# Recursive feature interaction on one core: the D groups moved ahead of c1, their copies shared by two engines, three tile loads put behind the D stores, and a lead of 7 chunks

## The chip, the cores and the metric

The kernel runs on one core of one Trainium2 chip. The metric is the device time of one execution in microseconds; less is better. The kernel before takes 185.95 us (median of 3 runs, 185.75 to 186.69).

## What is computed

The reference takes an input of 512 examples, 40 features and 16 dimensions, and three layers of weights. Each layer multiplies the input pairwise with the layer before and contracts the pairs with a weight tensor; the hidden rows of all three layers are summed over the 16 dimensions and go through one linear layer:

```python
base = inputs
curr = base
logit = []
for Wk, bk in zip(Ws, bs):
    z = jnp.einsum('bid,bjd->bdij', base, curr)
    curr = jnp.einsum('bdij,ijh->bhd', z, Wk) + bk[None, :, None]
    logit.append(curr)
pooled = jnp.sum(jnp.concatenate(logit, axis=1), axis=-1)
out = pooled @ lin_w + lin_b
```

Here `inputs` is 512 x 40 x 16, the weights are 40 x 40 x 100 and 40 x 100 x 100 (twice), and the output is 512 x 1.

## The kernel before

The columns (512 examples x 16 dimensions) are cut into 8 units of 1024 columns. Within a unit the products of pairs of features, `z`, are made in 7 chunks of 126 rows each, so there are 56 chunks, numbered m = 0 to 55. For each chunk VectorE (DVE) multiplies a tile `x_a` with a tile `x_b` into the buffer `xb_z` (function `form`), ScalarE (ACT) rounds it to `z_high` (`round_high`), and DVE takes the rest, `z_low` (`split`). TensorE (PE) then uses the chunk twice, each time in six matmuls of 512 columns: once with the weights `wc` (function `c1_chunk`, PSUM tiles `c1_ps`, called c_ps in the rows), once with the weights `wq` (`q_chunk`, PSUM tiles `q_ps`). Below, c7 is `c1_chunk` of chunk 7 and q0 is `q_chunk` of chunk 0. A split needs the rounded tile; c m needs both. For units 0 and 1 the program is written out; the later units run in hardware loops of two units.

The weights `wq` are not an input. Layers 2 and 3 are folded into them at the start: PE multiplies the last layer's weights into a vector `v` (`v_piece`, `turn_v`), then multiplies `w1_post` with it in five D groups (`d_group`, into two halves of the PSUM tile q_ps). Each group is copied to SBUF (`copy_d`, tile `w2_d`, called w_d in the rows), stored to memory in six transfers of the SP queue and one of GpSimd (POOL) (`store_d`, line L159), and read back in another layout in twelve gathers (`gather_d`, line L153) into `pair_sb`. Gathers of piece 0 hold the weights of chunks 0 and 1, those of piece 1 the chunks 2 to 6. Each piece is then added, rounded and split in three instructions per part (`first_weights` on DVE for chunks 0 and 1, lines L279 to L284; POOL for chunks 2 and 3 and for 4 to 6, lines L419 to L424).

In unit 0 the tiles `x_b` of chunks 1 to 6 are made by PE (`select_xb`); from unit 1 on they are loaded from memory by SP (`load_xb`, 512 KB each, line L171), each into the slot of `xb_z` that the split of seven chunks before has freed (semaphore `low_done`). Tile k of unit 1 belongs to chunk 7 + k.

Every engine executes its own stream in program order. SP's stream is the order in which its transfers are issued, and each semaphore wait in it holds back everything behind it. The constant `LAG` says how many chunks PE's c work is ahead of its q work: after the first `LAG` chunks of c, PE alternates q(m - LAG), c(m). Both kinds of chunk share 14 slots for `z`, which q frees.

Of the kernel before, what the change touches and what calls it, by code (L numbers as in the profile page):

```python
# [16 lines left out]
SLOTS = 2 * C  # L17
LAG = 8
BODY = 2 * C
PRODUCT_AT = 20  # L20
C1_AT = 3 * C - LAG

# [37 lines left out]
def build(nc, xa, xw, w0_pairs, w1x, w2h, small, out):  # L60
    fp32, f32r = mybir.dt.float32, mybir.dt.float32r
    ALU, ACT = mybir.AluOpType, mybir.ActivationFunctionType

    with ExitStack() as ctx:
# [3 lines left out]
        def sem(name):  # L68
            return ctx.enter_context(nc.semaphore(name))
# [96 lines left out]
        def _(sp):  # L166
# [3 lines left out]
            def load_xb(u, c):  # L170
                sp.dma_start(xb_z[:, c, :], xw[c:c + 128, bass.ds(u * N, N)]).then_inc(xb_loaded[c], 16)  # L171
# [47 lines left out]
            for c in range(4, C):  # L219
                sp.wait_ge(low_done, c + 1)  # L220
                load_xb(1, c)
# [13 lines left out]
        def _(dve):  # L235
# [38 lines left out]

            def first_weights():

                cols = slice(PREP_CUTS[0] * J, PREP_CUTS[1] * J)
                dve.wait_ge(dpair_loaded[0], 16 * sum(g[2] == 0 for g in GATHER))
                nc.vector.tensor_tensor(q_sides[0:K, 0, cols], q_sides[0:K, 0, cols], q_sides[0:K, 1, cols],  # L279
                                        ALU.add).then_inc(wq_sums, 1)  # L280
                dve.wait_ge(wq_sums, 1)
                nc.vector.tensor_copy(wq_high[0:K, cols], q_sides[0:K, 0, cols]).then_inc(wq_highs, 1)
                dve.wait_ge(wq_highs, 1)
# [35 lines left out]
        def _(act):  # L319
# [71 lines left out]
        def _(pool):  # L391
# [21 lines left out]
            for i in range(1, len(PREP_CUTS) - 1):
                cols = slice(PREP_CUTS[i] * J, PREP_CUTS[i + 1] * J)
                if PREP_CUTS[i] in WQ_CUTS:
                    piece = WQ_CUTS.index(PREP_CUTS[i])
                    pool.wait_ge(dpair_loaded[piece], 16 * sum(g[2] == piece for g in GATHER))
                    pool.wait_ge(wq_ready, 1)
                nc.gpsimd.tensor_tensor(q_sides[0:K, 0, cols], q_sides[0:K, 0, cols], q_sides[0:K, 1, cols],  # L419
                                        ALU.add).then_inc(wq_sums, 1)  # L420
                pool.wait_ge(wq_sums, i + 1)
                nc.gpsimd.tensor_copy(wq_high[0:K, cols], q_sides[0:K, 0, cols]).then_inc(wq_highs, 1)
                pool.wait_ge(wq_highs, i + 1)
                nc.gpsimd.tensor_tensor(wq_low[0:K, cols], q_sides[0:K, 0, cols], wq_high[0:K, cols].bitcast(fp32),  # L424
                                        ALU.subtract).then_inc(wq_ready, 1)

        @block.tensor
        def _(pe):
# [77 lines left out]
            def d_group(g):  # L506
# [130 lines left out]
```

## Time and profile before

| | |
|---|---|
| runs, median of 3 | 185.95 us |
| profiled execution, its own time | 186.29 us |
| its span, first to last instruction | 184.5 us |
| PE busy | 175.8 us (95%) |
| DVE busy | 151.8 us (82%) |
| ACT busy | 73.9 us (40%) |
| POOL busy | 16.2 us (9%) |

The span leaves 1.8 us of the execution's time outside of it. Busy time of PE is that of matmuls; the other engines work beside it. Times in the rows below are counted from the start of the span.

### The profile page before, as it was taken

What the parts mean: (1) busy time and instruction counts of PE and PEld (TensorE: products, weight loads), DVE (VectorE), ACT (ScalarE), POOL (GpSimd) and SP (SyncE); (2) the same over time, 40 slices, a digit from 0 to 9 for tenths busy, and PEclk for the clock granted to TensorE, in tenths of its full rate; (3) what the DMA queues carried; (4) which work ended last, traced back from release to release, by engine and by line L of the source; (5) the groups of instructions that cost most, each with busy time, mean ns of one, the idle gap of its engine ahead of it and who ended that gap; (6) DMA issues with size and microseconds to landing.
All of it is one profiled execution on the core that took longest, in us unless ns stands there. A gap on an engine that the chain in (4) does not pass through costs nothing.

```text
span 184.5 us, 2573 instructions
## 1 busy us (share of the span) xinstructions
PE 175.8 (95%) x814; PEld 118.7 (64%) x814; DVE 151.8 (82%) x135; ACT 73.9 (40%) x79; POOL 16.2 (9%) x21
## 2 busy tenths in 40 slices
PE   7798998869999999999999999999999999999994
PEld 2364474546677777777777777777777777777760
DVE  0699698869999999999999999999999999300622
ACT  2554664124444624462446244534453445002001
POOL 3670010087000000000000000000000000000000
PEclk9999999999999999999999999999999999999999
DMA  6999997999797739774986597659765200000000
GB/s 192 379 409 411 412 219 218 231 406 397 230 324 233 234 122 321 247 227 124 331 230 228 126 322 235 223 135 329 228 219 128 99 0 0 0 0 4 0 0 0
DMA packets 11845, 37.71 MB, mean 204 GB/s; under 512 B 2305, under 2 KB 2941, under 8 KB 11838
## 3 DMA queue, kind: packets, MB, share of 16 engines
q1 hardware_dynamic: 11538, 37.38, 62.1%
q0 software_dynamic: 48, 0.16, 0.3%
q10 hardware_dynamic: 252, 0.09, 0.3%
q8 instruction: 4, 0.07, 0.2%
q14 instruction: 3, 0.02, 0.0%
HBM read 36.28 MB, written 1.33 MB: 204 GB/s over the span
## 4 chain that ended last, share of the span: by engine, by line
PE 79%; DMA 8%; SPq 3%; POOL 3%; issue 2%; DVE 1%; ACT 1%; DVEq 0%; ACTq 0%
PE q_ps L434 39%; PE c_ps L434 36%; DMA pair_sb<-d_dram 3%; DMA pair_sb<-w_pairs 3%; DMA d_dram<-w_d 2%; PE q_ps L518 2%; SPq L153 2%; POOL pair_sb L401 1%; POOL wq_low L424 1%; PE q_ps L443 1%; POOL wc_low L406 1%; DVE xb_z L246 1%; ACT z_high L324 1%; SPq L159 1%; PE c_ps L565 1%
## 5 line engine op out<-in xcount | busy, mean ns | idle before, releaser
L324 ACT ACTIVATE z_high<-xb_z 126x1024 fp32r<-126x1024 f32 x56 | 59.2, 1060 | 73.0 <-DVE xb_z L246 69.3
L253 DVE TENSOR_TENSOR z_low<-xb_z,z_high 126x1024 fp32r<-126x1024 f32 x56 | 68.9, 1232 | 1.1 <-ACT z_high L324 0.8
L246 DVE TENSOR_TENSOR xb_z<-x_a,xb_z 126x1024 f32<-126x1024 f32 x50 | 62.1, 1242 | 8.3 <-DMA xb_z<-xw 8.3
L434 PE MATMUL q_ps<-z_high,wq_high 126*101 126x512 f32 x108 | 34.1, 396 | 3.0 <-POOL wq_low L424 1.5
L434 PE MATMUL c_ps<-z_high,wc_high 126*101 126x512 f32 x112 | 35.5, 398 | 0.2 <-issue 0.2
L434 PE MATMUL c_ps<-z_high,wc_low 126*101 126x512 f32 x112 | 35.0, 394 | 0.0
L434 PE MATMUL c_ps<-z_low,wc_high 126*101 126x512 f32 x112 | 35.0, 394 | 0.0
L434 PE MATMUL q_ps<-z_high,wq_low 126*101 126x512 f32 x108 | 33.8, 394 | 0.0
L434 PE MATMUL q_ps<-z_low,wq_high 126*101 126x512 f32 x108 | 33.7, 393 | 0.0
L434 PEld LDWEIGHTS q_ps<-z_high,wq_high 126*101 126x101 f32 x108 | 17.7, 165 | 10.8 <-POOL wq_low L424 2.0
L434 PEld LDWEIGHTS c_ps<-z_high,wc_high 126*101 126x101 f32 x112 | 18.0, 165 | 9.0 <-issue 1.6
L434 PEld LDWEIGHTS c_ps<-z_high,wc_low 126*101 126x101 f32 x112 | 18.5, 165 | 7.5
L434 PEld LDWEIGHTS c_ps<-z_low,wc_high 126*101 126x101 f32 x112 | 18.5, 165 | 7.4
L434 PEld LDWEIGHTS q_ps<-z_high,wq_low 126*101 126x101 f32 x108 | 17.9, 166 | 7.3
L434 PEld LDWEIGHTS q_ps<-z_low,wq_high 126*101 126x101 f32 x108 | 17.8, 165 | 7.2
L261 DVE TENSOR_TENSOR w_post<-q_ps,w_post 101x1024 f32<-101x1024 f32 x7 | 8.5, 1216 | 12.0 <-PE q_ps L434 12.0
L331 ACT ACTIVATE w_post<-c_ps 101x1024 f32<-101x1024 f32 x8 | 8.1, 1010 | 14.1 <-PE c_ps L434 14.1
L263 DVE TENSOR_TENSOR acc<-acc,w_post 101x1024 f32<-101x1024 f32 x7 | 8.6, 1226 | 0.2
L485 PE MATMUL q_ps<-warm_sb 128*128 128x512 bf16 x20 | 6.2, 483 | 1.4 <-POOL warm_sb L393 1.4
L267 DVE TENSOR_TENSOR w_post<-q_ps,w_post 101x256 f32<-101x256 f32 (+1 forms) x3 | 1.4, 508 | 5.2 <-PE q_ps L443 5.2
L388 ACT ACTIVATE out_sb<-c_ps,const_sb 1x512 f32<-1x512 f32 x1 | 0.7, 678 | 12.2 <-PE c_ps L568 12.2
L485 PEld LDWEIGHTS q_ps<-warm_sb 128*128 128x128 bf16 x20 | 2.3, 121 | 4.7 <-issue 2.2
(56 smaller groups left out, 66.1 us busy)
## 6 DMA issues: line engine op xcount, KB each, us to landing
xb_z<-xw SPq DMA_DIRECT2D x50, 512.0 KB, 4.5
x_a<-xa SPq DMA_DIRECT2D x8, 512.0 KB, 5.0
w_d<-w2h SPq DMA_DIRECT2D x4, 512.0 KB, 7.4
w_post<-w1x SPq DMA_DIRECT2D x3, 512.0 KB, 10.0
d_dram<-w_d SPq DMA_DIRECT2D x4, 252.5 KB, 4.3
w_post<-w1x SPq DMA_DIRECT2D x1, 562.5 KB, 12.7
pair_sb<-d_dram SPq DMA_DIRECT2D x6, 82.9 KB
pair_sb<-w_pairs SPq DMA_DIRECT2D x1, 404.0 KB, 5.4
```

The lines of the kernel that those rows point to most:

```text
L153: eng.dma_start(q_sides[P * t:P * (t + 1), side, c0 * J:c1 * J].rearrange("p (c j) -> p c j", j=J), src).then_inc(dpair_loaded[piece], 16)
L159: eng.dma_start(d_dram[r0:r1, column * J:(column + n) * J], w2_d[DR * upper + r0:DR * upper + r1, first * J:(first + n) * J]).then_inc(sto ...
L246: nc.vector.tensor_tensor(xb_z[0:K, c, :], x_a[0:K, u % 2, :], x_b, ALU.mult).then_inc(z_done, 1)
L253: nc.vector.tensor_tensor(z_low[0:K, m % SLOTS, :], xb_z[0:K, c, :], z_high[0:K, m % SLOTS, :].bitcast(fp32), ALU.subtract).then_inc(low_d ...
L261: nc.vector.tensor_tensor(prod, q_ps[u % 2][0:J, :], c1_sb[u % 2], ALU.mult).then_inc(q_psum_free, 1)
L263: nc.vector.tensor_tensor(acc[:, :], acc[:, :], prod, ALU.add).then_inc(acc_done, 1)
L324: nc.scalar.activation(z_high[0:K, m % SLOTS, :], xb_z[0:K, m % C, :], ACT.Copy).then_inc(high_done, 1)
L331: nc.scalar.activation(c1_sb[u % 2], c1_ps[u % 2][0:J, :], ACT.Copy).then_inc(c1_copied, 1)
L401: nc.gpsimd.tensor_tensor(side[:, :, 0, :], side[:, :, 0, :], side[:, :, 1, :], ALU.add).then_inc(wc_sums, 1)
L434: last = nc.tensor.matmul(ps[0:J, h * B:(h + 1) * B], w[0:K, c * J:(c + 1) * J], z[0:K, slot, h * B:(h + 1) * B], start=(c == 0 and k == 0 ...
L485: nc.tensor.matmul(warm_ps, warm_sb[:, 0:128], warm_sb[:, :], start=True, stop=True)
L518: last = nc.tensor.matmul(d_ps[g % 2][0:DR, 0:n], v_sb[:, :], w1_post[0:J, first:first + n], start=True, stop=True)
```

## The change

Six things change together.

1. PE: the D groups 0 to 4 stand ahead of c1; `select_xb(6)` stands between groups 1 and 2 instead of ahead of group 4.
2. The copies of groups 1 and 3 go from ACT to DVE (`copy_d` of DVE), with a semaphore of its own; all that waited for `dgroup_copied` now waits for both.
3. SP: tiles 0 and 1 of unit 1, which stood ahead of the D stores, come behind them: tile 0 behind the last store, tile 1 where tile 3 was (ahead of the gathers of piece 1), tile 2 between the third and the fourth gather of piece 1, tile 3 behind them.
4. `LAG` is 7 instead of 8: c0 to c6, then q0, c7, q1, c8, q2, c9 and so on.
5. DVE: the split of chunk 6 stands ahead of the form of chunk 7, `first_weights(0)` ahead of the split of chunk 7 (before: ahead of the split of chunk 8), and the weights of chunks 2 and 3 are made by DVE too (`first_weights(1)`), behind the split of chunk 8, which stands behind the form of chunk 9. POOL keeps the weights of chunks 4 to 6 alone.
6. ACT issues its three gathers ahead of the rounding of chunk 7 instead of chunk 8.

```diff
-LAG = 8
+LAG = 7
-C1_AT = 3 * C - LAG
+C1_AT = 2 * C - 1
-PREP_AT = 9
-GATHER_AT = 8
+PREP_AT = (7, 9)
+GATHER_AT = 7
...
             load_xa(1, 1)
-            for c in range(2):
-                sp.wait_ge(low_done, c + 1)
-                load_xb(1, c)
-            sp.wait_ge(dgroup_copied, 2)
+            sp.wait_ge(dgroup_copied, 1)
+            sp.wait_ge(dgroup_copied_dve, 1)
             store_d(sp, 0, LEFT, 0, 2 * GI, d_stored)
...
             store_d(sp, 0, LEFT + 4 * GI, 4 * GI, LOWER - 4 * GI, d_stored)
-            sp.wait_ge(low_done, 3)
-            load_xb(1, 2)
+            sp.wait_ge(low_done, 1)
+            load_xb(1, 0)
...
                 if piece == 1 and (side, t) == (0, 0):
-                    sp.wait_ge(low_done, 4)
-                    load_xb(1, 3)
+                    sp.wait_ge(low_done, 2)
+                    load_xb(1, 1)
+                if piece == 1 and (side, t) == (1, 1):
+                    sp.wait_ge(low_done, 3)
+                    load_xb(1, 2)
...
+            def copy_d(g):
+                dve.wait_ge(dgroup_done, g + 1)
+                nc.vector.tensor_copy(w2_d[:, g * GI * J:(g + 1) * GI * J], d_ps[g % 2]).then_inc(dgroup_copied_dve, 1)
...
                 for m in range(m0, m0 + BODY):
+                    if m == 5:
+                        copy_d(1)
+                    if m == C:
+                        split(it, C - 1)
                     form(it, m)
+                    if m == 5:
+                        copy_d(3)
...
-                    if m == PREP_AT:
-                        first_weights()
-                    if m > 1:
+                    if m == PREP_AT[0]:
+                        first_weights(0)
+                        split(it, C)
+                    elif m > 1 and m != C + 1:
                         split(it, m - 1)
+                    if m == PREP_AT[1]:
+                        first_weights(1)
...
             d_group(0)
             d_group(1)
-            c1_chunk(0, 1)
+            select_xb(6)
             d_group(2)
             d_group(3)
-            select_xb(6)
             d_group(4)
-            for m in range(2, LAG):
+            for m in range(1, LAG):
                 c1_chunk(0, m)
```

SP's stream before, from the second load of `x_a` to the last tile of unit 1 (xb_z<-xw is a tile load, d_dram<-w_d a store, pair_sb<-d_dram a gather):

```order
L168 DMA x_a<-xa 128x1024
L171 DMA xb_z<-xw 128x1024 x2
L159 DMA d_dram<-w_d 64x1010 x2
L159 DMA d_dram<-w_d 32x909
L159 DMA d_dram<-w_d 64x1010 x2
L159 DMA d_dram<-w_d 64x101
L171 DMA xb_z<-xw 128x1024
L153 DMA pair_sb<-d_dram 42x202 x3
L171 DMA xb_z<-xw 128x1024
L153 DMA pair_sb<-d_dram 42x505
L153 DMA pair_sb<-d_dram 42x5x101
```

The same place of SP's stream in the changed kernel, up to the fourth gather of piece 1 (line numbers are those of the changed kernel):

```order
L170 DMA x_a<-xa 128x1024
L161 DMA d_dram<-w_d 64x1010 x2
L161 DMA d_dram<-w_d 32x909
L161 DMA d_dram<-w_d 64x1010 x2
L161 DMA d_dram<-w_d 64x101
L173 DMA xb_z<-xw 128x1024
L155 DMA pair_sb<-d_dram 42x202 x3
L173 DMA xb_z<-xw 128x1024
L155 DMA pair_sb<-d_dram 42x505
L155 DMA pair_sb<-d_dram 42x5x101
L155 DMA pair_sb<-d_dram 42x505
L173 DMA xb_z<-xw 128x1024
```

Before, four tiles of unit 1 (0 to 3) stand ahead of the gathers of piece 1; now there are two (0 and 1) and a third (tile 2) in the middle of them.

DVE's stream before, from the form of chunk 7 to the form of chunk 11 (L246 is a form, L253 a split, L279 to L284 the weights of chunks 0 and 1):

```order
L246 TENSOR_TENSOR xb_z<-x_a,xb_z 126x1024
L253 TENSOR_TENSOR z_low<-xb_z,z_high 126x1024
L246 TENSOR_TENSOR xb_z<-x_a,xb_z 126x1024
L253 TENSOR_TENSOR z_low<-xb_z,z_high 126x1024
L246 TENSOR_TENSOR xb_z<-x_a,xb_z 126x1024
L279 TENSOR_TENSOR pair_sb<-pair_sb 126x202
L282 CAST wq_high<-pair_sb 126x202
L284 TENSOR_TENSOR wq_low<-pair_sb,wq_high 126x202
L253 TENSOR_TENSOR z_low<-xb_z,z_high 126x1024
L246 TENSOR_TENSOR xb_z<-x_a,xb_z 126x1024
L253 TENSOR_TENSOR z_low<-xb_z,z_high 126x1024
L246 TENSOR_TENSOR xb_z<-x_a,xb_z 126x1024
```

DVE's stream in the changed kernel, from the form of chunk 7 to the split of chunk 9 (L250 is a form, L257 a split, L287 to L292 weights):

```order
L250 TENSOR_TENSOR xb_z<-x_a,xb_z 126x1024
L287 TENSOR_TENSOR pair_sb<-pair_sb 126x202
L290 CAST wq_high<-pair_sb 126x202
L292 TENSOR_TENSOR wq_low<-pair_sb,wq_high 126x202
L257 TENSOR_TENSOR z_low<-xb_z,z_high 126x1024
L250 TENSOR_TENSOR xb_z<-x_a,xb_z 126x1024 x2
L257 TENSOR_TENSOR z_low<-xb_z,z_high 126x1024
L287 TENSOR_TENSOR pair_sb<-pair_sb 126x202
L290 CAST wq_high<-pair_sb 126x202
L292 TENSOR_TENSOR wq_low<-pair_sb,wq_high 126x202
L250 TENSOR_TENSOR xb_z<-x_a,xb_z 126x1024
L257 TENSOR_TENSOR z_low<-xb_z,z_high 126x1024
```

The forms of chunks 8 and 9 now stand together, ahead of the split of chunk 8, and the second set of weights stands between that split and the form of chunk 10.

## Rows read from the trace of the kernel before

**Rows 1.** The page: span, engines (busy us, share, instructions)

```profile
span 184.5 us, 2573 instructions
PE 175.8 (95%) x814; PEld 118.7 (64%) x814; DVE 151.8 (82%) x135; ACT 73.9 (40%) x79; POOL 16.2 (9%) x21
```

**Rows 2.** The chain that ended last: start, us, what

```profile
23.51 4.53 DMA d_dram<-w_d
...
32.04 5.49 DMA pair_sb<-d_dram
...
38.71 1.68 POOL wq_low L424
...
57.70 1.39 PE q_ps L434 x6
```

**Rows 3.** Timeline of PE: start, us, what, count [idle before, releaser]

```profile
18.27 0.70 PE L434 MATMUL c_ps<-z_high,wc_high 126*101 126x512 f32 x2
...
19.80 0.64 PE L518 MATMUL q_ps<-w_post,v_sb 101*64 101x505 f32 x1
...
21.65 0.73 PE L476 MATMUL q_ps<-z_high,select_r 126*128 126x512 f32 x2
22.31 0.39 PE L518 MATMUL q_ps<-w_post,v_sb 101*64 101x101 f32 x2
...
29.98 0.69 PE L434 MATMUL c_ps<-z_high,wc_high 126*101 126x512 f32 x2 [0.18 <-issue]
...
33.10 0.70 PE L434 MATMUL q_ps<-z_high,wq_high 126*101 126x512 f32 x2 [1.50 <-DVE wq_low L284]
...
40.44 0.71 PE L434 MATMUL q_ps<-z_high,wq_high 126*101 126x512 f32 x2 [1.50 <-POOL wq_low L424]
...
47.69 0.68 PE L434 MATMUL c_ps<-z_high,wc_high 126*101 126x512 f32 x2
```

**Rows 4.** Timeline of DVE

```profile
17.48 1.23 DVE L253 TENSOR_TENSOR z_low<-xb_z,z_high 126x1024 fp32r<-126x1024 f32 x1
18.63 1.21 DVE L246 TENSOR_TENSOR xb_z<-x_a,c_ps 126x1024 f32<-126x1024 f32 x1
...
31.88 0.37 DVE L279 TENSOR_TENSOR pair_sb<-pair_sb 126x202 f32<-126x202 f32 x1 [0.87 <-DMA pair_sb<-d_dram]
...
32.88 1.22 DVE L253 TENSOR_TENSOR z_low<-xb_z,z_high 126x1024 fp32r<-126x1024 f32 x1
34.78 1.23 DVE L246 TENSOR_TENSOR xb_z<-x_a,xb_z 126x1024 f32<-126x1024 f32 x1 [0.69 <-DMA xb_z<-xw]
...
41.39 1.87 DVE L246 TENSOR_TENSOR xb_z<-x_a,xb_z 126x1024 f32<-126x1024 f32 x1
```

**Rows 5.** Timeline of ACT: the copy of D group 3

```profile
21.77 0.59 ACT L338 ACTIVATE w_d<-q_ps 128x505 f32<-128x505 f32 x1 [0.26 <-PE q_ps L521]
```

**Rows 6.** Timeline of POOL

```profile
40.35 1.82 POOL L419 TENSOR_TENSOR pair_sb<-pair_sb 126x303 f32<-126x303 f32 x1
```

**Rows 7.** Timeline of SP's issues: start of the first, us to the last's end, what, count

```profile
24.20 0.58 SPq L171 DMA_DIRECT2D xb_z<-xw  x1
28.11 1.19 SPq L153 DMA_DIRECT2D pair_sb<-d_dram  x3
29.34 0.37 SPq L171 DMA_DIRECT2D xb_z<-xw  x1
29.76 2.67 SPq L153 DMA_DIRECT2D pair_sb<-d_dram  x6
```

**Rows 8.** Line L159, the store issued at 22.38: time from issue to landing

```profile
DMA to landing us min/median/max: 3.5/3.5/3.5
```

**Rows 9.** Line L171, tile 3 of unit 1, issued at 29.34: issue to landing

```profile
DMA to landing us min/median/max: 5.3/5.3/5.3
```

**Rows 10.** Line L171, tile 4 of unit 1, issued at 32.47: issue to landing

```profile
DMA to landing us min/median/max: 6.1/6.1/6.1
```

**Rows 11.** Line L171, tile 5 of unit 1, issued at 32.91: issue to landing

```profile
DMA to landing us min/median/max: 7.0/7.0/7.0
```

More of the change, by code:

```diff
@@ L202, in _ @@
             store_d(sp, 0, LEFT + F, 0, RIGHT, d_stored, (32, DR))
-            sp.wait_ge(dgroup_copied, 4)
+            sp.wait_ge(dgroup_copied, 2)
+            sp.wait_ge(dgroup_copied_dve, 2)
             store_d(sp, 0, LEFT + 2 * GI, 2 * GI, 2 * GI, d_stored)
             store_d(sp, 1, LEFT + LOWER + 2 * GI, 2 * GI, 2 * GI, d_stored)
-            sp.wait_ge(dgroup_copied, NG)
+            sp.wait_ge(dgroup_copied, 3)
             store_d(sp, 0, LEFT + 4 * GI, 4 * GI, LOWER - 4 * GI, d_stored)
-            sp.wait_ge(low_done, 3)
-            load_xb(1, 2)
+            sp.wait_ge(low_done, 1)
+            load_xb(1, 0)
             sp.wait_ge(equals_cleared, 1)
@@ L214, in _ @@
                 if piece == 1 and (side, t) == (0, 0):
-                    sp.wait_ge(low_done, 4)
-                    load_xb(1, 3)
+                    sp.wait_ge(low_done, 2)
[3 more added lines that the diff above has]
+                    load_xb(1, 2)
                 if side == 0 or piece > 0:
                     gather_d(sp, side, t, piece)
-            for c in range(4, C):
+            for c in range(3, C):
                 sp.wait_ge(low_done, c + 1)
@@ L273, in split_x, with first_weights @@
                                         ALU.subtract).then_inc(xa_split, 1)
-            def first_weights():
-                cols = slice(PREP_CUTS[0] * J, PREP_CUTS[1] * J)
-                dve.wait_ge(dpair_loaded[0], 16 * sum(g[2] == 0 for g in GATHER))
+            def copy_d(g):
+                dve.wait_ge(dgroup_done, g + 1)
+                nc.vector.tensor_copy(w2_d[:, g * GI * J:(g + 1) * GI * J], d_ps[g % 2]).then_inc(dgroup_copied_dve, 1)
+            def first_weights(i):
+                cols = slice(PREP_CUTS[i] * J, PREP_CUTS[i + 1] * J)
+                dve.wait_ge(dpair_loaded[i], 16 * sum(g[2] == i for g in GATHER))
                 nc.vector.tensor_tensor(q_sides[0:K, 0, cols], q_sides[0:K, 0, cols], q_sides[0:K, 1, cols],
                                         ALU.add).then_inc(wq_sums, 1)
-                dve.wait_ge(wq_sums, 1)
+                dve.wait_ge(wq_sums, i + 1)
                 nc.vector.tensor_copy(wq_high[0:K, cols], q_sides[0:K, 0, cols]).then_inc(wq_highs, 1)
-                dve.wait_ge(wq_highs, 1)
+                dve.wait_ge(wq_highs, i + 1)
                 nc.vector.tensor_tensor(wq_low[0:K, cols], q_sides[0:K, 0, cols], wq_high[0:K, cols].bitcast(fp32),
@@ L360, in _ @@
             copy_d(0)
-            copy_d(1)
             round_high(0, 4)
             copy_d(2)
-            copy_d(3)
             copy_d(4)
-            act.wait_ge(dgroup_copied, NG)
+            act.wait_ge(dgroup_copied, 3)
+            act.wait_ge(dgroup_copied_dve, 2)
             for m in range(5, BODY):
@@ L410, in _ @@
             pool.wait_ge(equals_cleared, 1)
-            pool.wait_ge(dgroup_copied, 4)
+            pool.wait_ge(dgroup_copied, 2)
+            pool.wait_ge(dgroup_copied_dve, 2)
             store_d(pool, 1, 0, UPPER - LEFT, LEFT, d_stored_pool, (0, 32))
[L413 to L425, printed above, removed]
+            cols = slice(PREP_CUTS[2] * J, PREP_CUTS[3] * J)
+            pool.wait_ge(dpair_loaded[1], 16 * sum(g[2] == 1 for g in GATHER))
+            nc.gpsimd.tensor_tensor(q_sides[0:K, 0, cols], q_sides[0:K, 0, cols], q_sides[0:K, 1, cols],
+                                    ALU.add).then_inc(last_sums, 1)
+            pool.wait_ge(last_sums, 1)
+            nc.gpsimd.tensor_copy(wq_high[0:K, cols], q_sides[0:K, 0, cols]).then_inc(last_highs, 1)
+            pool.wait_ge(last_highs, 1)
+            nc.gpsimd.tensor_tensor(wq_low[0:K, cols], q_sides[0:K, 0, cols], wq_high[0:K, cols].bitcast(fp32),
+                                    ALU.subtract).then_inc(last_ready, 1)
         @block.tensor
@@ L460, in q_chunk @@
                 u, c = divmod(m, C)
-                if m in PREP_CUTS[:-1]:
+                if m in PREP_CUTS[:2]:
                     pe.wait_ge(wq_ready, PREP_CUTS.index(m) + 1)
+                if m == PREP_CUTS[2]:
+                    pe.wait_ge(last_ready, 1)
                 if c == 0:
@@ L513, in d_group @@
                     pe.wait_ge(w1_loaded[W1_CUTS.index(g)], 16)
-                if g >= 2:
-                    pe.wait_ge(dgroup_copied, g - 1)
+                if g in (2, 4):
+                    pe.wait_ge(dgroup_copied, g // 2)
+                if g == 3:
+                    pe.wait_ge(dgroup_copied_dve, 1)
                 n = (GI if g < NG - 1 else 1) * J
```

2 lines of the change are left out of this document (added).

## Prediction

> **What bounds the kernel now.** I read the page first: PE is busy for 175.8 of 184.5 us [rows 1], so PE's own work is the bound, and only its gaps can be won. The chain that ended last [rows 2] shows where they are: from 40.44 on it is nothing but PE, chunk behind chunk at 1.39 us, and ahead of that it runs through the D stores (23.51 to 28.04), the gathers of piece 1 (32.04 to 37.53) and POOL's weights. PE's timeline [rows 3] gives the two gaps that matter: 1.50 us ahead of q0 at 33.10 and 1.50 ahead of q2 at 40.44. The gap ahead of c7 is 0.18, so c6 ended at 29.80. Behind 40.44 PE loses only crumbs: c12 starts at 47.69, five chunks later, 7.25 us where 5 x 1.39 are 6.95.
>
> Nothing in the change alters the amount of PE work. So I ask only when PE gets to which chunk. A lead of 7 has its own marks: at q0 one chunk of c less is done than before (c7), so the new kernel is level with the old one when q0 starts at 33.10 - 1.39 = 31.71, c8 at 40.44 - 2 x 1.39 = 37.66, and q2 at 39.05. For c9 I count back from c12, whose mark is 47.69 + 1.39 = 49.08: six chunks (c9, q3, c10, q4, c11, q5) are 8.34, so the mark of c9 is **40.74**. What PE is late there is late at the end.
>
> **D groups.** c1 costs 19.80 - 18.27 = 1.53 us of PE and goes behind the groups; the selection for chunk 6 costs 22.31 - 21.65 = 0.66 and stands now ahead of group 2 [rows 3]. So groups 2 and 3 come 0.87 earlier, and c6 still ends at 29.80, since the same things are done by then. Group 3's copy started at 21.77 and took 0.59 [rows 5]; now it can start at 20.90, on DVE. The trace has no copy of 505 columns on DVE; the bounds are 0.37 (202 columns) and 1.21 (1024 columns) [rows 4], and a straight line between them gives 0.68, which I take. It ends at 21.58 instead of 22.36: 0.78 earlier (1.1 to 0.25 by the bounds). The copy of group 1 stands where the form of chunk 5 started (18.63) and pushes it by 0.7, which is hidden: c5 is needed near 27. ACT loses two copies and has idle time anyway.
>
> **D stores.** The last store's landing ended the wait at 28.04. Two tiles, 1 MB, no longer stand ahead of the stores. That helps the first three, but the gathers wait for the last, issued after group 3's copy. The first store behind that copy landed 3.5 us after its issue [rows 8], the last 4.53 after the end of its own [rows 2], because three others go beside it. Nothing in the change thins these, so I shift the last landing by 0.78 only: the gathers start at 28.11 - 0.78 = 27.33 [rows 7]. If the last store too landed 3.5 after its issue, they would start at 26.3; if the copies gain only 0.25, at 27.9.
>
> **First weights and q0.** Before, gathers at 28.11 gave a landing at 31.88 (3.77 later), DVE's three instructions took 1.00 until its next one, and PE started 1.22 after the landing [rows 3, 4]. Now: landing 31.10, q0 at **32.32**. That is 0.61 behind its mark of 31.71, a wait of 2.5 us where 1.5 stood: the gain of 0.78 doesn't pay for the chunk c7 that no longer fills the hole. c7 runs behind q0; its split ends near 33.3, in time. Tile 0 takes tile 2's place in the queue (24.20 - 0.78, landed near 28.7 with the 5.3 of rows 9); DVE has time for chunk 7's form before 31.10.
>
> **The tiles.** This is the larger term. Tile 1 stands where tile 3 stood: issued at 29.34 - 0.78 = 28.56, and with its 5.3 [rows 9] landed at 33.86. Before, tile 3 landed at 34.64, the six gathers of piece 1 at 37.53, tile 4 at 38.57 and tile 5 at 39.91 [rows 2, 7, 9 to 11]. So six gathers cost 2.89 behind a tile, and a tile 1.0 to 1.3. Now tile 2 comes behind three gathers: 33.86 + 1.45 + 1.3 = 36.6 if the queue is strictly one behind the other, and 33.86 + 1.3 = 35.2 if the gathers run beside it. Some of tile 3's 5.3 was such overlap, so I take the middle, **35.9**. Piece 1 then lands near 37.4 to 38.1, no earlier than before: its issue gains 0.78 and loses a tile.
>
> The Trainium skill (DMA: Bandwidth & Descriptors, Queues, rings and completion order) says that each DMA engine takes the descriptors of one queue in the order of the ring. By that rule tile 2 can't pass the three gathers, 36.6 would hold, and the loss below would be 2.0 instead of 1.3 us; the landings here fit it but don't decide between the two.
>
> **DVE behind the tiles.** In its stream form 8, form 9, split 8, the second weights, form 10 and split 9 stand in this order. Form 9 needs tile 2, and c8 needs split 8 behind it. A form or split costs 1.15 from start to start, the weights 1.00 [rows 4]. From tile 2's landing: form 9 and split 8 2.3 (c8 at 38.3, against its mark of 37.66), weights 1.0, form 10 and split 9 2.3, and 0.1 until PE starts: c9 5.7 after tile 2. At 35.9 that is 41.6. q2 is done by then (38.3 + 2 x 1.39 = 41.1), so the splits decide.
>
> **POOL beside DVE.** POOL begins the weights of chunks 4 to 6 as soon as piece 1 has landed, with the addition of 303 columns (1.82 us [rows 6]), while DVE does the second weights and form 10. In the old trace a form beside that instruction took 1.87 instead of 1.21 [rows 4]. I charge 0.4 on the path, between nothing and twice 0.66. c9 starts at **42.0**, 1.26 us behind its mark.
>
> Here the Trainium skill (SBUF — State Buffer, Who interferes with whom) has a stricter rule: a VectorE instruction with two SBUF inputs and a GpSimd one that reads SBUF exclude each other for the whole of one instruction. By it DVE could lose up to 1.8 in one piece instead of 0.66, and the loss would grow to about 2.7. The 1.87 us form is slower, but less than that.
>
> **Behind c9.** DVE makes a chunk in 2.3 us, PE uses one in 2.78, so DVE gets ahead again and nothing more is lost. POOL has lost the smaller part of its weights (202 of 505 columns) and starts the rest at once, so q4 doesn't wait. At the end seven chunks of q follow the last c instead of eight; PE's sum is the same. DVE's five added instructions (two copies, three for the weights of chunks 2 and 3) all fall into the start and are counted above.
>
> **Sum.** +1.26 us, rounded to +1.25. The profiled execution took 186.29 against 184.5 of span; it is 0.34 above the median of 185.95. The forecast is on the median: 185.95 + 1.25 = **187.2 us**. A measurement of this kernel can tell about 0.5%, 0.93 us, from no change.
>
> **The rivals.**
>
> - *Same, chance 0.34.* Tile 2 is not far behind tile 1: at 35.2 c9 comes at 40.9, with POOL's 0.4 at 41.3, 0.56 late, 186.5 us. All of tile 2's landings from 34.1 to 35.2 or so end within 0.93 us. For it speaks that gathers of short rows may leave the queue free for tiles; against it, that tile 3 before took 5.3 with fewer gathers ahead of it. That the stores come no earlier (gathers at 27.9) belongs to the slower side, at about 187.8.
> - *Faster, chance 0.14.* The mechanism is the emptied queue: without the 1 MB ahead, every store lands 3.5 after issue, the gathers start at 26.3 and piece 0 lands at 30.07. Tile 1 is then issued at 27.5 and lands at 32.8; tile 2 1.0 later at 33.8, and piece 1 at 30.07 + 5.65 = 35.7, if the extra tile fits into the idle time of the DMA engines. c9 comes at 39.5, 1.2 before its mark: 184.7 us. It decides from tile 2 landed by 34.1 on. Against it: the last stores waited for each other, not for the tiles.
> - *Slower, chance 0.52.* The forecast, with tile 2 from 35.6 to 36.6 or later, 186.9 to 188.6 us; its upper end holds the exclusive lock too.
>
> The range leaves out most of the faster case and the rarest mishaps: 185.1 to 188.7.
>
> **What would show it.** D stores: the last copy on DVE ends near 21.6, the gathers start near 27.3. q0 starts near 32.3 behind a wait of 2.5. DVE waits for tiles ahead of form 8 (33.9) and form 9 (35.9), and PE waits ahead of c8 and c9 for DVE, not ahead of q2 for POOL. The prediction is wrong if the gathers start before 26.5 or form 9 before 34.2; then the gain of the early D groups reaches PE. It is also wrong, upward, if PE's longer waits lower its granted clock, of which the old trace shows nothing.

## The result, and the profile after

The changed kernel takes **189.0 us** (median of 4 runs, 188.62 to 189.32) against 186.32 us for the kernel before (median of 4 runs, 185.75 to 187.09): the ratio is 1.014, 95% interval 1.0093 to 1.0188. The profiled execution took 189.32 us with a span of 187.5, so 3.0 us more span than before. The sign was forecast, the size wasn't: 2.7 us instead of 1.25, and 189.0 us, where 187.2 was forecast, lies above the range of 185.1 to 188.7.

From the page of the changed kernel, the lines that answer to [rows 1], and the granted clock in 40 slices:

```profile
span 187.5 us, 2572 instructions
PE 177.8 (95%) x814; PEld 119.9 (64%) x814; DVE 153.2 (82%) x140; ACT 72.8 (39%) x77; POOL 11.4 (6%) x18
PEclk9999999699999999999999999999999999999999
```

PE's busy time has grown by 2.0 us with the same 814 matmuls, and the eighth slice of the clock (32.8 to 37.5 us) shows a 6. PE's timeline in the changed kernel, D group 3, then the first row of q0, c7, c8, q2, c9 and c12, to be held against [rows 3]:

```profile
20.50 0.64 PE L535 MATMUL q_ps<-w_post,v_sb 101*64 101x505 f32 x1 [0.19 <-DMA w_post<-w1x]
...
32.95 1.01 PE L447 MATMUL q_ps<-z_high,wq_high 126*101 126x512 f32 x2 [2.69 <-DVE wq_low L292]
...
35.46 1.06 PE L447 MATMUL c_ps<-z_high,wc_high 126*101 126x512 f32 x2
...
39.15 0.68 PE L447 MATMUL c_ps<-z_high,wc_high 126*101 126x512 f32 x2 [0.23 <-DVE z_low L257]
...
41.40 0.70 PE L447 MATMUL q_ps<-z_high,wq_high 126*101 126x512 f32 x2 [0.64 <-DVE wq_low L292]
...
43.76 0.68 PE L447 MATMUL c_ps<-z_high,wc_high 126*101 126x512 f32 x2 [0.75 <-DVE z_low L257]
...
52.11 0.62 PE L447 MATMUL c_ps<-z_high,wc_high 126*101 126x512 f32 x2
```

c9 starts at 43.76; its mark was 40.74, so PE is 3.02 us behind there, and the span ends 3.0 us later: behind c9 nothing more is lost (c12 at 52.11, 3.03 behind its mark of 49.08). Of this, 0.30 us is there before any of PE's work differs: PE starts D group 0 at 16.73 in this profile and at 16.43 in that of the kernel before. It is probably no work of the change, since e3 below, with the same streams up to that point, starts it at 16.11. Without it c9 is 2.72 late, and the medians differ by 2.7. The rest of the loss is made ahead of c9, and the last brackets name DVE: its weights ahead of q0 and q2, its splits ahead of c8 and c9.

DVE's timeline in the changed kernel (L250 forms, L257 splits, L281 the copies of D groups, L287 to L292 weights), to be held against [rows 4]:

```profile
21.62 0.68 DVE L281 COPY w_d<-q_ps 128x505 f32<-128x505 f32 x1 [0.88 <-PE q_ps L538]
...
31.73 0.37 DVE L287 TENSOR_TENSOR pair_sb<-pair_sb 126x202 f32<-126x202 f32 x1 [1.01 <-DMA pair_sb<-d_dram]
...
33.86 1.22 DVE L250 TENSOR_TENSOR xb_z<-x_a,xb_z 126x1024 f32<-126x1024 f32 x1
36.64 1.22 DVE L250 TENSOR_TENSOR xb_z<-x_a,xb_z 126x1024 f32<-126x1024 f32 x1 [1.56 <-DMA xb_z<-xw]
37.78 1.22 DVE L257 TENSOR_TENSOR z_low<-xb_z,z_high 126x1024 fp32r<-126x1024 f32 x1
38.91 1.00 DVE L287 TENSOR_TENSOR pair_sb<-pair_sb 126x202 f32<-126x202 f32 x1
39.95 0.38 DVE L290 CAST wq_high<-pair_sb 126x202 fp32r<-126x202 f32 x1
40.36 0.98 DVE L292 TENSOR_TENSOR wq_low<-pair_sb,wq_high 126x202 fp32r<-126x202 f32 x1
41.27 1.21 DVE L250 TENSOR_TENSOR xb_z<-x_a,xb_z 126x1024 f32<-126x1024 f32 x1
```

POOL's timeline beside it, for [rows 6], and SP's issues of the first gathers, for [rows 7]:

```profile
38.21 1.48 POOL L432 TENSOR_TENSOR pair_sb<-pair_sb 126x303 f32<-126x303 f32 x1 [14.64 <-DMA pair_sb<-d_dram]
39.75 0.46 POOL L435 CAST wq_high<-pair_sb 126x303 fp32r<-126x303 f32 x1
40.29 0.83 POOL L437 TENSOR_TENSOR wq_low<-pair_sb,wq_high 126x303 fp32r<-126x303 f32 x1
```

```profile
27.63 1.19 SPq L155 DMA_DIRECT2D pair_sb<-d_dram  x3
28.87 0.37 SPq L173 DMA_DIRECT2D xb_z<-xw  x1
```

Form 8 follows split 7 at once, where the text expected a wait for tile 1 until 33.9: tile 1, issued at 28.87, landed 4.5 us later at 33.4. Form 9 waits for tile 2 until 36.64, a split behind it, and then come the second weights: the same three instructions that take 0.99 us to the next one at 31.73 take 2.36 (38.91 to 41.27), with POOL's three beside them. Tile 2's issue at 30.62 and its landing:

```profile
L173 SPq DMA_DIRECT2D xb_z<-xw x1: 371/371/371, 30.6 to 30.6; - x1
...
DMA to landing us min/median/max: 5.9/5.9/5.9
```

The clock is in the busy times by stretch (busy us of PE, PEld, DVE, ACT, POOL, then granted clock, DMA share, GB/s):

```profile
30.00:33.00 3.00, 0.31 (x3) 0.06 (x1) 1.92 (x5) 1.06 (x1) 0.00 (x0) 1.00 0.87 259
33.00:36.00 3.00, 3.00 (x8) 2.03 (x9) 2.08 (x2) 0.89 (x1) 0.00 (x0) 0.53 1.05 265
36.00:37.00 1.00, 1.00 (x5) 0.72 (x4) 0.36 (x1) 0.17 (x1) 0.00 (x0) 0.71 1.11 174
```

After the wait of 2.69 us the granted clock is 0.50, that is 1.2 GHz, from 33.2 until about 36.6. q0 and c7 together take 4.41 us (32.95 to 37.36) instead of 2.78. Two explanations stand: **the DVE theory** (tile 2 and the slowed weights set c9, and the clock's loss falls into a wait) and **the clock theory** (the 1.63 us of q0 and c7 are the missing part of the loss).

### The profile page after: what moved, and what is told of

Same layout as the page of the kernel before. It is cut to its first block, busy times and chain, and to the rows that moved or that the text cites. A ratio compares the mean times of both kernels' runs of the same rounds, so it can differ in the third digit from the quotient of the medians.

```text
span 187.5 us, 2572 instructions
## 1 busy us (share of the span) xinstructions
PE 177.8 (95%) x814; PEld 119.9 (64%) x814; DVE 153.2 (82%) x140; ACT 72.8 (39%) x77; POOL 11.4 (6%) x18
## 4 chain that ended last, share of the span: by engine, by line
PE 75%; DMA 13%; SPq 6%; DVE 2%; issue 1%; ACT 0%; DVEq 0%
PE q_ps L447 38%; PE c_ps L447 35%; DMA w_post<-w1x 7%; DMA xb_z<-xw 4%; DMA d_dram<-w_d 2%; SPq L155 2%; SPq L181 1%; SPq L185 1%; SPq L173 1%; PE q_ps L456 1%; SPq L177 1%; DVE xb_z L250 1%; DVE z_low L257 1%; PE q_ps L535 1%; SPq L161 1%
## 5 line engine op out<-in xcount | busy, mean ns | idle before, releaser
L250 DVE TENSOR_TENSOR xb_z<-x_a,xb_z 126x1024 f32<-126x1024 f32 x50 | 61.0, 1219 | 10.1 <-DMA xb_z<-xw 10.1
L257 DVE TENSOR_TENSOR z_low<-xb_z,z_high 126x1024 fp32r<-126x1024 f32 x56 | 68.4, 1224 | 0.9 <-ACT z_high L341 0.9
L500 PE MATMUL q_ps<-warm_sb 128*128 128x512 bf16 x20 | 6.7, 512 | 1.4 <-POOL warm_sb L409 1.4
```

Source lines behind the costliest of these rows:

```text
L250: nc.vector.tensor_tensor(xb_z[0:K, c, :], x_a[0:K, u % 2, :], x_b, ALU.mult).then_inc(z_done, 1)
L257: nc.vector.tensor_tensor(z_low[0:K, m % SLOTS, :], xb_z[0:K, c, :], z_high[0:K, m % SLOTS, :].bitcast(fp32), ALU.subtract).then_inc(low_d ...
L500: nc.tensor.matmul(warm_ps, warm_sb[:, 0:128], warm_sb[:, :], start=True, stop=True)
```

## The experiments

Each ran beside the kernel before on the same chip; "ratio" is to that kernel, with its 95% interval. Reading single microseconds from one profile needs care: c2 starts anywhere from 22.36 to 23.34 in them, and D group 0, which stands ahead of everything that differs on PE, anywhere from 16.11 to 16.73 (16.43 before). Where two are compared, I count from c2's start, and for the D groups from the start of group 0.

### e3_fill_clock: PE kept at work through the wait

```diff
             for m in range(1, LAG):
                 c1_chunk(0, m)
+            pe.wait_ge(dgroup_copied, 3)
+            pe.wait_ge(dgroup_copied_dve, 2)
+            for _ in range(FILL):          # 10
+                warm()
```

> The changed kernel with ten added matmuls on zeros (2.2 us of work, into PSUM that is free then) between c6 and q0, so that PE doesn't stand still for 2.7 us. Theory: the clock stays at 2.4 GHz, q0 to q1 end 1.6 us earlier, but c8 still waits for split 8 until 39.1 and the end doesn't move (within 0.4 us). Rival (clock): the time falls by 1.6 us to about 187.4.

Measured: 188.79 us, ratio 1.0164 (1.0116 to 1.0213). The clock stayed at 1.00 in the whole span and q0 and c7 took 2.96 us instead of 4.41. PE's and DVE's timelines show where that went:

```profile
37.94 0.68 PE L448 MATMUL c_ps<-z_high,wc_high 126*101 126x512 f32 x2 [1.94 <-DVE z_low L258]
```

```profile
35.43 1.23 DVE L251 TENSOR_TENSOR xb_z<-x_a,xb_z 126x1024 f32<-126x1024 f32 x1 [1.59 <-DMA xb_z<-xw]
36.57 1.22 DVE L258 TENSOR_TENSOR z_low<-xb_z,z_high 126x1024 fp32r<-126x1024 f32 x1
37.71 1.00 DVE L288 TENSOR_TENSOR pair_sb<-pair_sb 126x202 f32<-126x202 f32 x1
```

What q0 and c7 won is a wait of 1.94 us ahead of c8, for the same split behind the same tile. The 1.6 us that the clock theory promised are not in the time. From c2 to c9 it is 20.02 us instead of 20.61, but tile 2 landed 0.6 us earlier in this profile too (5.2 us after its issue at 30.14). The mean clock was 1.00 in three of the six executions (188.18, 188.35 and 189.08 us) and 0.99 in the others (188.50, 189.17 and 190.42), where all four of the changed kernel have 0.99; too few to price it to some tenths. e1 below, with the clock up and no gain either, says the same: the clock theory is out as the missing part of the loss.

### e2_tile2_ahead: tile 2 ahead of all gathers of piece 1

```diff
                 if piece == 1 and (side, t) == (0, 0):
                     sp.wait_ge(low_done, 2)
                     load_xb(1, 1)
-                if piece == 1 and (side, t) == (1, 1):
                     sp.wait_ge(low_done, 3)
                     load_xb(1, 2)
```

> The changed kernel; tile 2 is issued right behind tile 1, ahead of all six gathers of piece 1. Theory: tile 2 lands near 34.8 instead of 36.5, split 8 ends near 37.2, and then the gathers' landing (38.2, unchanged) holds DVE's second weights; c9 comes near 43.0, 0.7 us earlier, time about 188.3. Rival (clock): c8 can't start before q1 ends at 38.9, so nothing at c8; a gain of at most 0.25 us.

Measured: 188.5 us, ratio 1.0147 (1.0095 to 1.0199). Form 9 no longer waits: forms 8 and 9 run from 34.28 to 36.63 and split 8 starts at 36.62, and from c2 to c9 it is 19.44 us (23.19 to 42.63) instead of 20.61. That gain of 1.17 us is hardly in the time, whose interval holds the changed kernel's ratio. It moves the profile as the DVE theory says; the time alone doesn't prove it. POOL and DVE begin their additions side by side here:

```profile
37.71 0.84 POOL L431 TENSOR_TENSOR pair_sb<-pair_sb 126x303 f32<-126x303 f32 x1 [14.09 <-DMA pair_sb<-d_dram]
```

```profile
37.77 1.01 DVE L286 TENSOR_TENSOR pair_sb<-pair_sb 126x202 f32<-126x202 f32 x1
```

### e1_serial_weights: POOL waits until DVE's second weights are done

```diff
             pool.wait_ge(dpair_loaded[1], 16 * sum(g[2] == 1 for g in GATHER))
+            pool.wait_ge(wq_ready, 2)
```

> The changed kernel; POOL's weights of chunks 4 to 6 wait until DVE's second weights are done. Theory (DVE's chain behind tile 2 sets c9, and POOL beside it costs 1.36 us on the second weights): those three instructions take 1.0 us again instead of 2.36, POOL's work then falls beside form 10 and split 9 and slows them by 0.4 to 0.9, so c9 starts 0.5 to 1.0 us earlier than in the changed kernel (43.76) and the time falls by as much, to about 188.2. Rival (PE's clock at its lower level after the long wait is what costs): no change of the time, since q0 and its wait are as before.

Measured: 189.15 us, ratio 1.0169 (1.0125 to 1.0214), no gain. DVE's and POOL's timelines:

```profile
38.40 0.36 DVE L287 TENSOR_TENSOR pair_sb<-pair_sb 126x202 f32<-126x202 f32 x1
38.80 0.27 DVE L290 CAST wq_high<-pair_sb 126x202 fp32r<-126x202 f32 x1
39.10 0.37 DVE L292 TENSOR_TENSOR wq_low<-pair_sb,wq_high 126x202 fp32r<-126x202 f32 x1
39.38 1.22 DVE L250 TENSOR_TENSOR xb_z<-x_a,xb_z 126x1024 f32<-126x1024 f32 x1
40.52 1.86 DVE L257 TENSOR_TENSOR z_low<-xb_z,z_high 126x1024 fp32r<-126x1024 f32 x1
42.30 1.45 DVE L250 TENSOR_TENSOR xb_z<-x_a,xb_z 126x1024 f32<-126x1024 f32 x1
43.67 1.86 DVE L257 TENSOR_TENSOR z_low<-xb_z,z_high 126x1024 fp32r<-126x1024 f32 x1
```

```profile
39.63 1.67 POOL L433 TENSOR_TENSOR pair_sb<-pair_sb 126x303 f32<-126x303 f32 x1 [16.84 <-DVE wq_low L292]
41.36 1.31 POOL L436 CAST wq_high<-pair_sb 126x303 fp32r<-126x303 f32 x1
42.75 1.70 POOL L438 TENSOR_TENSOR wq_low<-pair_sb,wq_high 126x303 fp32r<-126x303 f32 x1
```

The first half of the expectation held: alone, the weights take 0.98 us to the next instruction. But POOL's work then lies beside the splits, and three long instructions give back 0.65 + 0.24 + 0.65 = 1.54 us (over 1.21). From c2 to c12 it is 28.94 us (22.36 to 51.30), in the changed kernel 28.96. So POOL's 303 columns cost DVE 1.4 to 1.5 us in either place; DVE has no idle time in either. The clock stayed at 1.00 in this profile, behind a wait of 2.19 us ahead of q0 and one of 2.55 ahead of c8, and q0 and c7 took 2.89 us: that didn't make the kernel faster either.

### e7_pool_weights: POOL makes the weights of chunks 2 and 3 again

```diff
-                    if m == PREP_AT[1]:
-                        first_weights(1)
...
+            low = slice(PREP_CUTS[1] * J, PREP_CUTS[2] * J)
+            nc.gpsimd.tensor_tensor(q_sides[0:K, 0, low], q_sides[0:K, 0, low], q_sides[0:K, 1, low],
...
```

> The changed kernel with the weights of chunks 2 and 3 made by POOL again, ahead of those of chunks 4 to 6. Theory: DVE saves the 2.36 us of its second weights, form 10 starts when tile 3 has landed (39.3), and POOL's longer work slows form 10 and the splits by some 1.5 us in all; c9 near 42.8, time 0.5 to 1.0 us below the changed kernel. Rival (q2 waits longer for POOL): q2 not before 41.5 and no gain.

Measured: 188.82 us, ratio 1.0118 (1.0067 to 1.017). The rival was the nearer: q2 starts at 42.95, behind a wait of 1.68 us for POOL, in a profile that is the longest of the six executions (189.91 us; the shortest took 187.18). The interval holds the changed kernel's ratio, so neither a gain nor a loss from this part, undone alone, is shown.

### e5_tiles_back: the tiles issued as before

```diff
+            for c in range(2):
+                sp.wait_ge(low_done, c + 1)
+                load_xb(1, c)
             sp.wait_ge(dgroup_copied, 1)
...
-            sp.wait_ge(low_done, 1)
-            load_xb(1, 0)
+            sp.wait_ge(low_done, 3)
+            load_xb(1, 2)
...
-                    sp.wait_ge(low_done, 2)
-                    load_xb(1, 1)
+                    sp.wait_ge(low_done, 4)
+                    load_xb(1, 3)
```

(Tile 2 in the middle of the gathers goes too; the loop behind them starts at tile 4.)

> The changed kernel with the tiles of unit 1 issued as before: 0 and 1 ahead of the stores, 2 behind them, 3 ahead of piece 1. Theory (the tiles' new place is the larger loss): DVE no longer waits for tiles ahead of form 8 and form 9, split 8 ends near 37, c9 starts near 41.0, and the time is within 0.7 us of the kernel before, 186.5. Rival (the lead of 7 or the order of DVE's work is the loss): time stays at 188 or above.

Measured: 187.35 us, ratio 1.0086 (1.0052 to 1.0121). PE's waits in it:

```profile
32.33 0.70 PE L447 MATMUL q_ps<-z_high,wq_high 126*101 126x512 f32 x2 [1.89 <-DVE wq_low L292]
...
41.59 0.68 PE L447 MATMUL c_ps<-z_high,wc_high 126*101 126x512 f32 x2 [0.50 <-DVE z_low L257]
```

DVE doesn't wait for tiles, split 8 ends at 36.82, and c9 starts 0.85 behind its mark; the span is 185.4, 0.9 above before. The theory had 186.5 us, the rival 188 or more; the time lies between. Put back, the tiles take 0.54% off the ratio's 1.4%, about 1.0 us, though the two intervals overlap; in the two profiles c9 comes 2.2 us earlier. It is the largest gain of the parts that I undid alone, but a loss of 0.86% remains. The slowed weights are still there:

```profile
36.73 1.00 DVE L287 TENSOR_TENSOR pair_sb<-pair_sb 126x202 f32<-126x202 f32 x1
```

The next form starts at 39.09, 2.36 us behind this row. From 31.12, where the first weights start, to the end of split 9 at 41.44 DVE never stops, so here its own work sets c9. How the 0.86% divides between the lead and the weights no run shows.

### e6_lead8: a lead of 8 in the changed kernel

```diff
-LAG = 7
+LAG = 8
```

> The changed kernel with a lead of 8. Theory: the lead of 7 limits the damage of the late tiles. With 8, c7 must come ahead of q0 and waits for its split (near 34), and c9 stands ahead of q2 and waits for split 9 (43.7) with one chunk less done; the time is 1.4 us above the changed kernel, about 190.4. Rival (the lead is neutral, or a loss of its own): the same as the changed kernel within 0.4 us, or less.

Measured: 190.29 us, ratio 1.0226 (1.0183 to 1.027), as expected (190.4). c7 starts at 34.67 and c9, now ahead of q2, at 43.74 behind split 9. With the tiles late, the lead of 7 saves 1.3 us by the medians, 1.6 by the ratios.

### e9_lead7_alone: a lead of 7 in the kernel before

```diff
-LAG = 8
+LAG = 7
...
-C1_AT = 3 * C - LAG
+C1_AT = 2 * C - 1
```

> The kernel before with a lead of 7 and nothing else. Theory (the marks: at equal times of q0 and q2 a lead of 7 has one chunk less behind it): q0 still waits for the first weights until 33.1, now 2.9 us, q2 for POOL's until 40.4, and one chunk more is left then; 1.4 us slower, 187.3. PE's clock falls after the long wait, which is hidden ahead of q2. Rival (the lead only reorders PE's work and is neutral): within 0.4 us of before.

Measured: 186.94 us, ratio 1.0062 (1.0024 to 1.0101); 1.16 us, expected 1.4. PE's one long wait:

```profile
33.44 0.70 PE L434 MATMUL q_ps<-z_high,wq_high 126*101 126x512 f32 x2 [3.48 <-DVE wq_low L284]
```

The wait ahead of q0 is 3.48 us, and q2 starts at 40.65 where its mark is 39.05. It doesn't wait for POOL, as I had expected: the clock fell to 0.50 behind the long wait, and q0 to c8 took 7.21 us where four chunks at full clock are 5.56. POOL's weights were ready at 40.16, so at most some 0.5 us of the delay is the clock's and the rest would have been a wait. The rest of the kernel runs through. A chunk taken out of a hole comes back as most of a chunk of time at the end, as the marks say.

### e10_tiles_alone: the tiles' new places in the kernel before

```diff
-            for c in range(2):
-                sp.wait_ge(low_done, c + 1)
-                load_xb(1, c)
             sp.wait_ge(dgroup_copied, 2)
...
-            sp.wait_ge(low_done, 3)
-            load_xb(1, 2)
+            sp.wait_ge(low_done, 1)
+            load_xb(1, 0)
```

(Tiles 1 and 2 stand among the gathers as in the change.)

> The kernel before with the tiles in the changed kernel's places (0 behind the stores, 1 ahead of piece 1, 2 in the middle of it) and nothing else; the lead stays 8 and DVE's order is that of before. Theory: form 8 waits for tile 1 until 33.9 and split 7 stands behind it, so c7 comes near 36.2 instead of 29.98 and q0 behind it; form 9 waits for tile 2 until 36.6 with the first weights behind it. c12 comes 5 to 7 us late, time 191 to 193. Rival (tiles are hidden): within 1 us of before.

Measured: 191.09 us, ratio 1.0298 (1.0271 to 1.0324): 5.3 us slower. DVE's waits in it:

```profile
29.49 1.23 DVE L246 TENSOR_TENSOR xb_z<-x_a,xb_z 126x1024 f32<-126x1024 f32 x1 [3.94 <-DMA xb_z<-xw]
...
33.48 1.23 DVE L246 TENSOR_TENSOR xb_z<-x_a,xb_z 126x1024 f32<-126x1024 f32 x1 [1.62 <-DMA xb_z<-xw]
...
36.67 1.23 DVE L246 TENSOR_TENSOR xb_z<-x_a,xb_z 126x1024 f32<-126x1024 f32 x1 [0.83 <-DMA xb_z<-xw]
```

Forms 7, 8 and 9 wait for tiles 0, 1 and 2, with a split or the first weights queued behind each; c7 starts at 35.94 (expected 36.2). The tiles' places cost 3.0% here and 0.5% in the changed kernel (against e5), so the other parts take up most of their cost. The lead of 7 saves 1.3 to 1.6 us with the tiles late (e6) and costs 1.16 with the tiles in their old places (e9). The new order on DVE was never tried by itself, and its share is not shown.

### e4_groups_only: the D groups ahead and shared copies, in the kernel before

```diff
-            c1_chunk(0, 1)
+            select_xb(6)
             d_group(2)
             d_group(3)
-            select_xb(6)
             d_group(4)
-            for m in range(2, LAG):
+            for m in range(1, LAG):
```

(And the copies of groups 1 and 3 on DVE, as in the change.)

> The kernel before with the D groups ahead of c1 and their copies shared by ACT and DVE, nothing else changed. Theory: group 3 must wait for its part of w1_post, which lands near 20 to 20.5, so the last copies end within 0.3 us of before, the gathers start within 0.5 us of 28.1 and the time is that of before within 0.5 us. Rival (the prediction's step on the D groups): gathers 0.8 us earlier, and a gain of 0.5 to 0.8 us.

Measured: 185.48 us, ratio 0.9973 (0.9944 to 1.0003). DVE's copy of group 3 and SP's first gathers:

```profile
21.04 0.68 DVE L280 COPY w_d<-q_ps 128x505 f32<-128x505 f32 x1 [0.89 <-PE q_ps L534]
```

```profile
27.20 1.19 SPq L154 DMA_DIRECT2D pair_sb<-d_dram  x3
```

The copy starts 0.73 earlier than before and the gathers 0.91, but group 0 starts 0.29 earlier too (16.14). Counted from it, the copy is 0.44 earlier where 0.87 was forecast, since group 3 does wait 0.20 us for its part of `w1_post` (it starts at 19.92), and the gathers 0.62 where the prediction had 0.78 and I had expected 0.5 at most. The changed kernel is the same: its copy is 0.45 earlier and its gathers 0.78. Both expectations were half right. And the step is not safe: in four of the ten profiles with the D groups ahead (e5, e6, e7 and e11) group 2 waits for its part of `w1_post` as well, and the gathers start 11.54 to 12.02 us behind group 0, where it is 11.68 in the kernel before and 10.90 to 11.13 in the other six. The time's gain, 0.3%, is not clear of no change.

### e8_split10_first: in e4, the split of chunk 10 ahead of the form of chunk 11

```diff
+                    if m == SPLIT_FIRST:      # 11
+                        split(it, m - 1)
                     form(it, m)
...
-                    if m > 1:
+                    if m > 1 and m != SPLIT_FIRST:
                         split(it, m - 1)
```

> The kernel before with the D groups ahead of c1 and shared copies, as in e4_groups_only, and the split of chunk 10 ahead of the form of chunk 11, which waits for tile 4. Theory (a split queued behind a form that waits for a tile is what PE waits for): in e4_groups_only PE waited 1.05 us ahead of c10 and 0.35 ahead of c11; both go, c12 comes 1.2 to 1.4 us earlier than there, time about 184.2. Rival (POOL beside DVE slows the splits in any order): gain below 0.4 us, since c11 or c12 then waits instead.

Measured: 185.82 us, ratio 0.9983 (0.9956 to 1.0011), no gain where the theory had 184.2. c10 no longer waits for a split, but in this profile piece 1 landed 0.85 later than in that of e4 and q2 waited for POOL. The number is the rival's, the mechanism isn't. PE's row, and the busy times by stretch behind it:

```profile
39.89 0.71 PE L448 MATMUL q_ps<-z_high,wq_high 126*101 126x512 f32 x2 [1.83 <-POOL wq_low L438]
```

```profile
40.00:42.00 2.00, 2.00 (x7) 1.33 (x7) 2.00 (x2) 1.51 (x3) 1.94 (x2) 0.65 1.02 408
42.00:44.00 2.00, 2.00 (x6) 1.44 (x5) 2.00 (x3) 0.92 (x2) 1.92 (x2) 0.50 1.03 410
```

Here the clock fell as well, behind a wait, and this time nobody else was late (split 11, which c11 needs, ended at 42.7): q2 and c10 took 4.43 us (39.89 to 44.32) instead of 2.78, by the rows 1.65 us on the path. But this is the longest of twelve executions, 187.03 us, and ten of them have a mean clock of 0.999 or 1.00, so the fall explains this profile and not the median.

### e11_all_three: e8, and DVE makes the weights of chunks 2 and 3 between split 10 and form 11

```diff
                     if m == SPLIT_FIRST:
                         split(it, m - 1)
+                        first_weights(1)
...
-            for i in range(1, len(PREP_CUTS) - 1):
+            for i in range(2, len(PREP_CUTS) - 1):
...
+                pool.wait_ge(dpair_loaded[1], 16 * sum(g[2] == 1 for g in GATHER))
+                pool.wait_ge(wq_ready, 2)
```

> The kernel before with the D groups ahead and shared copies, split 10 ahead of form 11, DVE making the weights of chunks 2 and 3 between them while it would wait for tile 4, and POOL's weights of chunks 4 to 6 waiting for that. Theory: the weights take 1.0 us on DVE (no POOL beside), q2 starts about 1.3 us behind piece 1's landing instead of 3, near 38.3, PE is at work without a stop from q0 on but for some 0.5 us, its clock stays up; c12 at 46.0 to 46.4 against 47.69, time 184.2 to 184.8. Rival (POOL's slowing of the splits comes back behind it): c11 or c12 wait for splits, time 185.5 or more.

Measured: **183.92 us**, ratio 0.9914 (0.9883 to 0.9946), faster than both kernels. The profiled execution is the longest of the six, 185.55 us; four of the six took 183.68 to 184.0 and have no profile. PE's longer waits in it are those of 0.55 us ahead of q0, 0.65 and 0.49, and the clock stays at 1.00:

```profile
37.63 0.69 PE L447 MATMUL c_ps<-z_high,wc_high 126*101 126x512 f32 x2 [0.65 <-DVE z_low L257]
...
39.74 0.70 PE L447 MATMUL q_ps<-z_high,wq_high 126*101 126x512 f32 x2 [0.49 <-DVE wq_low L292]
```

c12 starts at 47.03 against 47.69 before, in a profile whose c2 is 0.56 later (23.19): 1.2 us gained behind c2. The early D groups have no part in that gain: group 2 waits for `w1_post`, and the gathers start at 28.17, 0.06 later than before. The weights are again on DVE, as in the change, but behind the split that PE needs, and POOL beside nothing urgent.

## Why the prediction was wrong, point by point

**The marks** held. The delay of c9 against 40.74 (3.02) is the difference of the spans (3.0), and e9 shows the price of the lead alone, 1.16 us for 1.39, some of it perhaps the clock's.

**D groups and stores.** Forecast 0.78 us earlier. In the profile of the changed kernel the gathers start at 27.63, 0.48 earlier, which is 0.78 counted from group 0; in e4 it is 0.62. The agreement is partly luck: the copy came only 0.45 earlier, since group 3 waited for its load, and the stores landed faster than forecast. The copy on DVE took 0.68, exactly the straight line between the bounds. I had not asked when `w1_post` lands once PE comes earlier: the next wait behind the one removed.

**q0.** Forecast 32.32, measured 32.95: the landing came 4.10 instead of 3.77 after the issue. It made no difference in the end: c8 waits for split 8 behind tile 2, and c9 for split 9.

**The tiles.** The mechanism was right and the size too small. Tile 1 landed at 33.4 (forecast 33.86), tile 2 at 36.5 (35.9; the strict order in the queue gave 36.6). That 36.5 is so near to 36.6 is partly luck, for tile 1 was 0.5 early: the step that I had to choose is that from tile 1's landing to tile 2's, between 1.3 and 2.75, and it measured 3.1 instead of the 2.04 that I took (2.8 to 3.8 in e1, e3, e6 and e7). The middle had no ground; by the Trainium skill's rule on one queue's ring (DMA: Bandwidth & Descriptors, Queues, rings and completion order) the upper bound was the value, and these landings agree with it and lie somewhat above it. By tile 2's landing it is 0.6 us of the miss, 0.3 of which is the later start of this profile.

**POOL beside DVE** is the step that failed. I charged 0.4 us "between nothing and twice 0.66", for long instructions. The instructions that met POOL were DVE's short ones: 0.37, 0.27 and 0.37 became 1.00, 0.38 and 0.98, together 1.36 more and just outside the upper bound of 1.32. The same three durations, within 0.01 us, stand in the profiles of e2, e3, e5 and e6, so this is no chance of one profile. The rows fit a lock, one engine waiting for the other's instruction to end, and not a slowing: in all five profiles DVE's addition ends 0.22 to 0.24 us behind the end of POOL's (39.91 and 39.69 here, 38.78 and 38.55 in e2), and its subtraction as much behind POOL's. That is the rule of the Trainium skill's SBUF — State Buffer (Who interferes with whom), and these traces agree with it. But the price that the prediction drew from it, up to 1.8 us in one piece, came from reading POOL's 1.82 us as POOL's work. POOL's addition took 1.82 us in e3, where it began inside a split of DVE, and 0.84 in e2, where it began 0.06 ahead of a short one: the longer time holds POOL's own wait for DVE. What DVE lost in one instruction was 0.63 us at the most here, and 0.65 in e1. 0.96 us of the miss.

**The sum:** 36.5 + 5.7 + 1.36 = 43.6 for c9, measured 43.76; 0.6 + 0.96 + 0.2 left over make 1.26 into 3.02. The 0.2 lies in small steps, such as 0.1 from the landing to form 9's start. c8's wait (0.23) and c9's (0.75) are where the text said; q2's wait of 0.64 is for DVE's weights, which I had put at none.

**The clock** was named as what could push the time up, and it did fall. But c9 waits for DVE all the same, and neither e3 nor e1, whose profiles have the clock at 1.00, is faster: by these it cost nothing that can be seen here.

What stays open: why group 0 starts anywhere from 16.11 to 16.73 (the load of `w1_post` moves with it: group 3, which waits for it, starts 3.77 us behind group 0 in the changed kernel and 3.78 in e4), and why in some executions group 2 waits for a load too; and how much of e11's gain the split's order and DVE's weights each have, since e4 and e8 alone are not clear of no change. The parts don't add up: alone, the lead costs 0.6%, the tiles' places 3.0% and the D groups gain 0.3% (not clear of no change), and together with the new order on DVE they cost 1.4%.

## What to carry to other kernels

When a hole of PE is filled or shortened, count which chunk stands at which time on both sides, not the length of the wait: work taken out of a hole comes back at the end. A form that waits for a transfer holds every split queued behind it, so the order on the vector engine has a say in what a late tile costs; put what PE needs next ahead of whatever waits for a load. Work on GpSimd beside a busy VectorE cost VectorE the same 1.4 to 1.5 us here in either order; look for a place where VectorE waits anyway. In the kernel before, POOL's first addition (202 columns, at 37.61) fell into DVE's wait of 1.55 us for tile 4 and took 0.61 us; whether moving all of it there would pay was not tried.

## What was not expected of the hardware

- TensorE's clock fell from 2.4 to 1.2 GHz in the changed kernel behind a wait of 2.69 us, for about 3.4 us. The length of the wait alone doesn't decide it: it fell behind waits of 1.83 us (e8), 1.89 (e5), 3.03 (e7), 3.08 (e2), 3.39 (e10), 3.48 (e9) and 4.27 (e6), and stayed up behind 1.50 twice (before), 1.94 (e3), and 2.19 and 2.55 (e1). So e3's ten small matmuls are not shown to be what kept it up.
- Whether the fall costs time depends on who else is late: nothing that can be seen in the changed kernel, 1.65 us by the rows of e8. The kernel before has it in some executions too: of 49 beside the experiments, 36 have a mean clock of 1.00 and a median of 185.7 us, 13 one of 0.99 and a median of 186.5; no run shows that the one comes from the other.
- DVE and POOL took turns by whole instructions where both added or subtracted tiles of SBUF: DVE's short instruction ended 0.22 to 0.24 us behind POOL's in five profiles.
- POOL's three instructions on 303 columns took 2.9 us beside DVE's short ones (38.21 to 41.12) and 4.8 us beside its long ones (39.63 to 44.45 in e1), and cost DVE about the same, 1.36 and 1.54 us.
